# A score store and a probability load as three transfers of 32 rows each

## The chip, the cores and the metric

The kernel runs on one core of a Trainium2 chip. A core has five engines that run their own instruction streams side by side: TensorE (PE, matrix products into PSUM), VectorE (DVE), ScalarE (ACT), GpSimd (POOL) and SyncE (SP), which here does nothing but issue DMA transfers and wait. They meet at semaphores. The metric is the device time of one execution in microseconds, lower is better. Before the change it was 2473.29 us, the median of 3 runs (2472.25 to 2475.6).

## The reference

Two cross-attention layers are applied to `x` of 64 batches, 256 positions, 320 channels, 20 heads of 16. Each batch has 77 context tokens of 512 features. Layer 0 uses all 77 as text. Layer 1 takes the first 73 as text and the last 4 as image tokens, whose scores get a cosine term. Cut to what matters here, in layer 1:

```python
q = heads(hidden_states @ W_q)
probs_t = softmax(q . (text @ W_k) * Dh ** -0.5)
text_out = probs_t @ (text @ W_v)
attn_scores = jnp.einsum('bhsd,bhnd->bhsn', q, k_ip) * attn_scale     # 4 image tokens
qsem = l2norm(jnp.einsum('bhst,bte->bhse', probs_t, text_ehs))
sem = jnp.einsum('bhse,bne->bhsn', qsem, l2norm(ip_ehs))
probs_ip = softmax(attn_scores + 0.5 * sem, axis=-1) * spatial_mask[None, None, :, None]
ip_out = jnp.einsum('bhsn,bhnd->bhsd', probs_ip, v_ip)
out = (text_out + ip_out) @ W_out + b_out + residual
```

## The kernel before, in words

A first stage computes keys, values and the products of context tokens for all batches and leaves them in device memory; it ends at about 337 us of the span. The second stage, the function `attention`, is a software pipeline over the 64 batches, written out in full. In each round every engine works through a fixed list of steps, the table `ORDER` (L124). A word such as `1pl/4` is step `pl` of layer 1, for the batch 4 rounds back. No scheduler moves anything at run time: an engine that waits holds all that stands behind it. PSUM banks are handed from use to use by the table `USES`.

The image tokens' path in layer 1 goes as follows. TensorE computes the scores of three groups of channels (`ip_scores`, L1048), each group 32 rows (8 heads times 4 tokens) by 256 positions. ScalarE writes them to `sipst`, 96 rows of 1 KB (L1147). The softmax needs another layout, 96 rows of (head and quarter of the positions) with the 4 tokens side by side, and the turn goes through device memory: SP stores `sipst` to `s_dram` (step `ss`, L886) and loads `sip` from there (step `sl`, L891). DVE runs the image softmax in 20 small steps (`ip_softmax`, L1204). The first (L1221) needs the norms that SP has loaded (`nl`), the last writes `pip` (L1262). SP stores `pip` to `p_dram` (step `ps`, L897) and loads it as `pt`, again three groups of 32 rows (step `pl`, L902). TensorE multiplies `pt` with the image values (`attend_ip`, L1064, products of L1070), and DVE adds that to the text's result (L1269).

Around these steps SP has, in a round: the layer-0 sums of the softmax, 4 rows of `ust` to the 96 rows of `den` (step `ds`, L840), the same for layer 1 behind `pl`, the keys and the Gram matrix, two stores of the inverses (`rw`, L865), four moves of the numerators within `ust` (`sh`, L855) and the spread of the inverses over 128 rows, `rb` (`rl`, L871). DVE's reciprocal (L1195) waits for `den`. GpSimd's product with the inverses (L1310) waits for `rb`. ScalarE rounds the product to 16 bits (`ah`, L1159), GpSimd takes the rest (`al`, L1315), and TensorE's output projection (L933) needs both. DVE adds the residual to it (L1280); in layer 0 that is `x1a` or `x1b`, the input of layer 1.

Of the kernel before, what the change touches and what calls it, by code (L numbers as in the profile page):

```python
# [16 lines left out]
B, S, C = 64, 256, 320  # L17
# [7 lines left out]
CW = 3  # L25
# [6 lines left out]
SLOT = 32  # L32
# [640 lines left out]
def attention(nc, psum, early, x, k_dram, v_dram, g_dram, c_dram, kip_dram, vip_dram, r_dram, n_dram, s_dram, p_dram,  # L673
# [3 lines left out]
    with ExitStack() as stack:  # L677
        def sb(name, shape, dt=F32):
            return stack.enter_context(nc.sbuf_tensor(name, shape, dt))

        def sem(name):
            return stack.enter_context(nc.semaphore(name))
# [36 lines left out]
        sipst = sb("sipst", [IPR, 2, S])  # L719
# [4 lines left out]
        pt = sb("pt", [IPR, S])  # L724
# [11 lines left out]
        s_ss, s_sl = sem("ip_scores_stored"), sem("ip_scores_loaded")  # L736
        s_ps, s_pt = sem("ip_probabilities_stored"), sem("ip_probabilities_loaded")
# [17 lines left out]
        def banks(l, use, n=1):  # L755
            r = turn_banks.bank(l, use)
            return psum[:, r:r + n, :]
# [4 lines left out]
        def wait_free(eng, l, b, *uses):  # L762
            turn_banks.wait(eng, freed, b, l, *uses)
# [31 lines left out]
        def _(sp):  # L795
# [89 lines left out]

            def store_ip_scores(l, b, n):  # L886
                b.reached(sp, s_sip, 1, 1)
                dst = s_dram[b.parity()].rearrange("m (c s) -> c m s", c=CW)
                sp.dma_start(dst, sipst[:, b.parity(), :]).then_inc(s_ss, 16)

            def load_ip_scores(l, b, n):  # L891
                b.reached(sp, s_y, STEPS, SIP_READ - STEPS)
                b.reached(sp, s_ss, 16, 16)
                src = s_dram[b.parity()].rearrange("(n h) (q i) -> (h q) n i", n=IP, i=QS)
                sp.dma_start(sip[:, b.parity(), :, :], src).then_inc(s_sl, 16)

# [4 lines left out]

            def load_ip_probabilities(l, b, n):  # L902
                b.reached(sp, s_ps, 16, 16)
                src = p_dram.rearrange("m (c s) -> c m s", c=CW)
                sp.dma_start(pt[:], src).then_inc(s_pt, 16)

            def store(l, b, n):
                b.reached(sp, s_xo[1], 1, 1)
# [4 lines left out]
                               "vi": load_vip, "ds": move_denominators, "d": move_semantics, "sh": move_numerators,  # L913
                               "rw": store_inverses, "rl": spread_inverses, "ns": store_norms, "nl": load_norms,
                               "ss": store_ip_scores, "sl": load_ip_scores, "ps": store_ip_probabilities,
                               "pl": load_ip_probabilities, "st": store})
            sp.wait_ge(s_store, 16 * B)

        @block.tensor
        def _(pe):  # L920
# [143 lines left out]
            def attend_ip(l, b, n):  # L1064
                wait_free(pe, l, b, "p")
                b.reached(pe, s_vb, 1, 1)
                b.reached(pe, s_pt, 16, 16)
                for c in range(CW):
                    rows = slice(c * SLOT, (c + 1) * SLOT)
                    mm = pe.matmul(banks(l, "p", 3)[:, c, 0:S], vb[rows, :, :].rearrange("p h d -> p (h d)"),  # L1070
                                   pt[rows, :], start=True, stop=True)
                mm.then_inc(f_p, 1)

            def output(l, b, n):
# [3 lines left out]

            program("pe", {"q": query, "s": scores, "m": turn_max, "t": turned_scores, "a": attend,
                               "u": gram_products, "n": square_norms, "i": ip_scores, "p": attend_ip, "o": output})  # L1080

        @block.scalar
# [416 lines left out]
```

## Time and profile before

| | |
|---|---|
| runs | 2473.29 us median (2472.25 to 2475.6) |
| profiled execution, its own time | 2473.34 us |
| its span | 2471.8 us |
| granted TensorE clock, mean | 0.98 |
| busy: PE, DVE, ACT, POOL | 92%, 69%, 70%, 64% |
| DMA: packets, bytes | 337787, 310.89 MB |

The span is what the profile covers; the 1.5 us between it and the execution's own time lie around it. TensorE is busy nearly all the time, but the end of its matmuls is modelled, and the other engines wait for it and it for them in turn. A share of busy time does not say what a change of one transfer is worth. For that one reads which wait ends last at a place.

### The profile page before, as it was taken

What the parts mean: (1) busy time and instruction counts of PE and PEld (TensorE: products, weight loads), DVE (VectorE), ACT (ScalarE), POOL (GpSimd) and SP (SyncE); (2) the same over time, 40 slices, a digit from 0 to 9 for tenths busy, and PEclk for the clock granted to TensorE, in tenths of its full rate; (3) what the DMA queues carried; (4) which work ended last, traced back from release to release, by engine and by line L of the source; (5) the groups of instructions that cost most, each with busy time, mean ns of one, the idle gap of its engine ahead of it and who ended that gap; (6) DMA issues with size and microseconds to landing.
All of it is one profiled execution on the core that took longest, in us unless ns stands there. A gap on an engine that the chain in (4) does not pass through costs nothing.

```text
span 2471.8 us, 90321 instructions
## 1 busy us (share of the span) xinstructions
PE 2273.8 (92%) x35896; PEld 1458.5 (59%) x35896; DVE 1699.8 (69%) x2860; ACT 1726.8 (70%) x2602; POOL 1593.7 (64%) x1056
## 2 busy tenths in 40 slices
PE   7899967999999999999999999999999999999984
PEld 5677744555555555556555555655556555556552
DVE  5534333777777777777777777777777777777763
ACT  3323325877777777778777778877787787787862
POOL 3212124777777777777777777777777777777762
PEclk9999978999999999999999999999999999999997
DMA  9677642444434444444444444444444444444431
GB/s 289 197 225 229 198 115 64 112 114 115 111 109 117 115 114 117 115 118 116 112 117 116 114 115 119 117 111 116 114 118 116 113 118 118 115 118 117 112 90 56
DMA packets 337787, 310.89 MB, mean 126 GB/s; under 512 B 180208, under 2 KB 280816, under 8 KB 337392
## 3 DMA queue, kind: packets, MB, share of 16 engines
q1 hardware_dynamic: 337392, 305.36, 44.0%
q8 instruction: 280, 4.59, 0.8%
q14 instruction: 115, 0.94, 0.1%
HBM read 164.66 MB, written 105.98 MB: 109 GB/s over the span
## 4 chain that ended last, share of the span: by engine, by line
PE 34%; DVE 18%; DMA 12%; ACT 8%; issue 6%; SPq 6%; POOL 1%; ACTq 0%; DVEq 0%; POOLq 0%
PE psum L933 8%; PE psum L1032 8%; DMA den<-ust 8%; PE psum L1016 6%; PE psum L995 5%; ACT ef L1121 5%; DVE mneg L1180 3%; DVE e L1202 2%; PE psum L936 2%; DVE sq L1221 2%; DVE ust L1269 2%; DVE outt L1280 2%; DMA pt<-p_dram 2%; PE psum L999 1%; PE psum L958 1%
## 5 line engine op out<-in xcount | busy, mean ns | idle before, releaser
L1348 POOL TENSOR_TENSOR e<-ef,eh 73x1024 f32<-73x1024 f32 x320 | 681.4, 2130 | 298.9 <-ACT eh L1136 261.9
L1121 ACT ACTIVATE ef<-psum 73x1024 f32<-73x1024 f32 (+1 forms) x640 | 628.5, 1012 | 104.8 <-PE psum L999 100.9
L1202 DVE TENSOR_TENSOR e<-psum,e 73x1024 f32<-73x1024 f32 x320 | 386.6, 1208 | 158.5 <-PE psum L1032 158.2
L1180 DVE TENSOR_REDUCE mneg<-psum 128x8 f16<-128x616 f32 (+3 forms) x512 | 448.2, 930 | 31.0 <-PE psum L958 30.2
L1032 PE MATMUL psum<-eh,gram 128*73 128x512 f16 x1280 | 337.6, 387 | 36.6 <-ACT ef L1121 12.7
L1016 PE MATMUL psum<-ef,values 128*32 128x256 f32 x5120 | 363.5, 389 | 8.0 <-DVE pip L1262 5.9
L995 PE MATMUL psum<-q_high,keys 32*73 32x256 f16 (+2 forms) x6144 | 325.5, 259 | 33.9 <-DVE mneg L1180 25.4
L1136 ACT ACTIVATE eh<-ef 73x1024 f16<-73x1024 f32 x320 | 337.0, 1053 | 16.4 <-ACT ef L1121 0.8
L995 PEld LDWEIGHTS psum<-q_high,keys 32*73 32x73 f16 (+1 forms) x6144 | 187.7, 111 | 143.6 <-issue 68.1
L1129 ACT ACTIVATE ust<-psum 128x512 f32<-128x512 f32 x384 | 228.2, 594 | 63.2 <-PE psum L1016 59.2
L1315 POOL TENSOR_TENSOR al<-ust,ah 128x768 f16<-128x768 f32 x128 | 210.7, 1646 | 86.6 <-ACT ah L1159 86.5
L1310 POOL TENSOR_TENSOR ust<-ust,rb 128x768 f32<-128x768 f32 x128 | 231.8, 1811 | 24.7 <-DMA rb<-r_dram 24.5
L1032 PEld LDWEIGHTS psum<-eh,gram 128*73 128x73 f16 x1280 | 121.5, 115 | 187.4 <-ACT ef L1121 43.8
L933 PE MATMUL psum<-ah,wo 128*128 128x256 f16 x1280 | 195.2, 276 | 16.0 <-POOL al L1315 15.8
L999 PE MATMUL psum<-mt,sel 32*73 32x256 f16 (+3 forms) x3072 | 205.7, 252 | 0.0
L995 PE MATMUL psum<-q_low,keys 32*73 32x256 f16 (+3 forms) x3072 | 205.7, 252 | 0.0
L1016 PEld LDWEIGHTS psum<-ef,values 128*32 128x32 f32 x5120 | 134.2, 110 | 113.8 <-issue 30.0
L1195 DVE RECIPROCAL rd<-den 96x64 f32<-96x64 f32 x128 | 69.7, 544 | 167.7 <-DMA den<-ust 163.4
L1044 PE MATMUL psum<-e,pick 128*32 128x256 f32 x2560 | 178.2, 388 | 3.0 <-DVE e L1202 3.0
L1187 DVE SCALAR_TENSOR_TENSOR q_low<-psum,q_high 128x640 f16<-128x640 f32 x128 | 102.2, 799 | 111.8 <-ACT q_high L1103 111.3
L933 PE MATMUL psum<-xh,wq 128*128 128x256 f16 x1024 | 156.3, 276 | 10.6 <-POOL xl L1305 4.7
L660 POOL TENSOR_TENSOR ch<-cx,one 128x2464 f16<-128x2464 f32 x7 | 30.0, 4292 | 194.4 <-PE psum L422 183.3
(180 smaller groups left out, 4659.7 us busy)
## 6 DMA issues: line engine op xcount, KB each, us to landing
rb<-r_dram SPq DMA_DIRECT2D x128, 384.0 KB, 3.8
keys<-k_dram SPq DMA_DIRECT2D x128, 231.0 KB, 3.7
values<-v_dram SPq DMA_DIRECT2D x128, 192.5 KB
ust<-ust SPq DMA_DIRECT2D x512, 48.0 KB, 2.1
v_dram<-vst SPq DMA_DIRECT2D x64, 320.0 KB
out<-outt SPq DMA_DIRECT2D x64, 320.0 KB, 2.3
k_dram<-kst SPq DMA_DIRECT2D x32, 616.0 KB, 3.9
x<-in_x SPq DMA_DIRECT2D x32, 384.0 KB, 3.7
```

Of the source, the lines that this page charges most:

```text
L933: mm = pe.matmul(o[:, c * S:(c + 1) * S], a, data[:, k, :], **at_ends)
L995: pe.matmul(o, keys(l, low, c)[rows, e, 0:n], q[rows, cols], start=(low == 0 and q is qh[l]), stop=False)
L999: mm = pe.matmul(o, sel[rows, k, 0:n], mt[l][rows, lead:lead + many], start=False, stop=True)
L1016: mm = pe.matmul(row(l, f"a{c}")[j * SLOT:(j + 1) * SLOT, r * S:(r + 1) * S], va[l][:, h, :], e, start=True, stop=True)
L1032: mm = pe.matmul(banks(l, f"u{k}", 2)[0:n, r, :], gm[:, half, :], e, start=(half == 0), stop=(half == 1))
L1121: act.activation(ef[l][0:m, unit_heads(n), :].rearrange("t h s -> t (h s)"), src, ACT.Exp, scale=SM).then_inc(s_exp[l], 1)
L1129: act.activation(ust[l][:, b.parity(), :, c, :], src, ACT.Copy).then_inc(s_u[l], 1)
L1136: act.activation(eh[0:m, unit_heads(k), :], ef[1][0:m, unit_heads(k), :], ACT.Copy, scale=0.5)\
L1180: dve.tensor_reduce(dst, o, AX_X, ALU.max, negate=True).then_inc(s_max[l], 1)
L1202: dve.tensor_tensor(rest, banks(l, f"u{k}", 2)[0:m, :, :], rest, ALU.mult).then_inc(s_wr, 1)
L1310: pool.tensor_tensor(at(l, b), at(l, b), rb[l][:], ALU.mult).then_inc(s_at[l], 1)
L1348: pool.tensor_tensor(e2[0:m, k, :, :], ef[1][0:m, unit_heads(k), :], eh[0:m, unit_heads(k), :], ALU.subtract).then_inc(s_e2, 1)
```

## The change

Where one transfer of three groups (in `s_dram` and `p_dram` a group is 256 of the 768 columns) stood, three transfers of 32 rows each stand. They raise the same semaphore, so its waits go by 48 in place of 16: in `load_ip_scores` on SP and in `attend_ip` on TensorE.

```diff
             def store_ip_scores(l, b, n):
                 b.reached(sp, s_sip, 1, 1)
-                dst = s_dram[b.parity()].rearrange("m (c s) -> c m s", c=CW)
-                sp.dma_start(dst, sipst[:, b.parity(), :]).then_inc(s_ss, 16)
+                for c in range(CW):
+                    sp.dma_start(s_dram[b.parity()][:, c * S:(c + 1) * S], sipst[c * SLOT:(c + 1) * SLOT, b.parity(), :])\
+                      .then_inc(s_ss, 16)
 
             def load_ip_scores(l, b, n):
                 b.reached(sp, s_y, STEPS, SIP_READ - STEPS)
-                b.reached(sp, s_ss, 16, 16)
+                b.reached(sp, s_ss, 16 * CW, 16 * CW)
...
             def load_ip_probabilities(l, b, n):
                 b.reached(sp, s_ps, 16, 16)
-                src = p_dram.rearrange("m (c s) -> c m s", c=CW)
-                sp.dma_start(pt[:], src).then_inc(s_pt, 16)
+                for c in range(CW):
+                    sp.dma_start(pt[c * SLOT:(c + 1) * SLOT, :], p_dram[:, c * S:(c + 1) * S]).then_inc(s_pt, 16)
...
             def attend_ip(l, b, n):
                 wait_free(pe, l, b, "p")
                 b.reached(pe, s_vb, 1, 1)
-                b.reached(pe, s_pt, 16, 16)
+                b.reached(pe, s_pt, 16 * CW, 16 * CW)
```

On SP, in a round of the loop, the score store stands between the values of layer 0 and the load of the scores, and before the change reads:

```order
L821 DMA values<-v_dram 77x640 [waits filled_a0]
L889 DMA s_dram<-sipst 3x32x256 [waits ip_scores_read]
L895 DMA sip<-s_dram 96x4x64 [waits ip_scores_stored,ip_softmax_steps]
L875 DMA rb<-r_dram_0 128x1x768 [waits inverses_stored1,text_attended1]
L862 DMA ust<-ust 16x768 [waits semantics_moved,denominators_moved1,text_attended1]
```

and after it:

```order
L821 DMA values<-v_dram 77x640 [waits filled_a0]
L889 DMA s_dram<-sipst 32x256 [waits ip_scores_read]
L889 DMA s_dram<-sipst 32x256 x2
L896 DMA sip<-s_dram 96x4x64 [waits ip_scores_stored,ip_softmax_steps]
L875 DMA rb<-r_dram_1 128x1x768 [waits inverses_stored1,text_attended1]
```

Nothing changes its place; two more transfers stand ahead of the load that waits for all three. Further down in the same round on SP, from the sums of layer 0 to the spread of its inverses (`rb`), before the change:

```order
L845 DMA den<-ust 96x1x64 [waits inverses0,sums_read0]
L821 DMA values<-v_dram 77x640 [waits filled_a1]
L905 DMA pt<-p_dram 96x1x256 [waits ip_probabilities_stored]
L845 DMA den<-ust 96x1x64 [waits inverses1,sums_read1]
L814 DMA keys<-k_dram 128x924 [waits filled_t0]
L828 DMA gram<-g_dram 77x146 [waits filled_u]
L869 DMA r_dram_1<-rd 8x12x64 [waits inverses0]
L869 DMA r_dram_1<-rd 8x12x64
L862 DMA ust<-ust 16x768 [waits denominators_moved0,text_attended0]
L862 DMA ust<-ust 16x768 x3
L875 DMA rb<-r_dram_1 128x1x768 [waits inverses_stored0,text_attended0]
```

and after it:

```order
L845 DMA den<-ust 96x1x64 [waits inverses0,sums_read0]
L821 DMA values<-v_dram 77x640 [waits filled_a1]
L906 DMA pt<-p_dram 32x256 [waits ip_probabilities_stored]
L906 DMA pt<-p_dram 32x256 x2
L845 DMA den<-ust 96x1x64 [waits inverses1,sums_read1]
L814 DMA keys<-k_dram 128x924 [waits filled_t0]
L828 DMA gram<-g_dram 77x146 [waits filled_u]
```

Here too the order stays, with two more transfers between the first of `pt` and the sums of layer 1; what stands behind them follows as before. On the other engines no instruction is added or moved.

## Rows read from the trace of the kernel before

**Rows 1.** The page: the chain that ended last, by line.
```profile
PE psum L933 8%; PE psum L1032 8%; DMA den<-ust 8%; PE psum L1016 6%; PE psum L995 5%; ACT ef L1121 5%; DVE mneg L1180 3%; DVE e L1202 2%; PE psum L936 2%; DVE sq L1221 2%; DVE ust L1269 2%; DVE outt L1280 2%; DMA pt<-p_dram 2%; PE psum L999 1%; PE psum L958 1%
```

**Rows 2.** Timeline of SP in one batch: start, duration, queue, line, transfer, count.
```profile
1513.23 0.64 SPq L845 DMA_DIRECT2D den<-ust  x1
...
1514.46 0.74 SPq L905 DMA_DIRECT2D pt<-p_dram  x1
1515.30 0.58 SPq L845 DMA_DIRECT2D den<-ust  x1
...
1518.41 2.49 SPq L862 DMA_DIRECT2D ust<-ust  x4
1521.00 0.56 SPq L875 DMA_DIRECT2D rb<-r_dram  x1
```

**Rows 3.** Timeline of DVE in that batch; in brackets the idle time before.
```profile
1515.56 0.54 DVE L1195 RECIPROCAL rd<-den 96x64 f32<-96x64 f32 x1
...
1519.60 0.55 DVE L1195 RECIPROCAL rd<-den 96x64 f32<-96x64 f32 x1 [2.42 <-DMA den<-ust]
...
1529.40 0.74 DVE L1221 TENSOR_SCALAR sq<-n 96x64 f32<-96x64 f32 x1
...
1533.53 0.96 DVE L1280 SCALAR_TENSOR_TENSOR x1a<-psum,res 128x768 f32<-128x768 f32 x1
```

**Rows 4.** Timeline of GpSimd (POOL) in that batch.
```profile
1525.54 1.80 POOL L1310 TENSOR_TENSOR ust<-ust,rb 128x768 f32<-128x768 f32 x1
1528.44 1.65 POOL L1315 TENSOR_TENSOR al<-ust,ah 128x768 f16<-128x768 f32 x1 [1.10 <-ACT ah L1159]
```

**Rows 5.** Timeline of ScalarE (ACT) in that batch.
```profile
1527.46 0.84 ACT L1159 ACTIVATE ah<-ust 128x768 f16<-128x768 f32 x1 [0.60 <-POOL ust L1310]
```

**Rows 6.** Line 1221 over the run: count, duration in ns min/median/max.
```profile
L1221 DVE TENSOR_SCALAR sq<-n x64: 180/847/2076, 443.4 to 2442.7; 96x64 f32<-96x64 f32 x64
```

**Rows 7.** Line 875 (rb) over the run: who waited (us, times), and its landings.
```profile
  POOL ust L1310: 24.5, 11
...
DMA to landing us min/median/max: 3.5/3.8/5.3
```

**Rows 8.** Issues of five kinds, ns min/median/max; last, the landings of L895.
```profile
L889 SPq DMA_DIRECT2D s_dram<-sipst x64: 759/780/822, 411.9 to 2421.3; - x64
L905 SPq DMA_DIRECT2D pt<-p_dram x64: 713/722/862, 459.2 to 2454.0; - x64
L862 SPq DMA_DIRECT2D ust<-ust x512: 507/589/1787, 366.6 to 2449.2; - x171
L798 SPq DMA_DIRECT2D kip<-kip_dram x2: 595/598/600, 337.4 to 338.0; - x2
L895 SPq DMA_DIRECT2D sip<-s_dram x64: 321/343/354, 416.6 to 2424.8; - x64
...
DMA to landing us min/median/max: 1.9/2.0/4.5
```

**Rows 9.** Busy time in one microsecond (columns: PE, PEld, DVE, ACT, POOL, clock, DMA, GB/s).
```profile
1504.00:1505.00 1.00, 1.00 (x20) 0.42 (x24) 1.00 (x2) 0.82 (x1) 1.00 (x1) 1.00 0.16 53
```

**Rows 10.** The chain that ended last, in order of time: start, us, what.
```profile
1515.30 4.17 DMA den<-ust
...
2421.28 3.42 DMA s_dram<-sipst
...
2453.99 4.14 DMA pt<-p_dram
```

**Rows 11.** SP's own waits over the run: us in total, times, longest us.
```profile
SPq L121 <- DMA s_dram<-sipst: 198.7, 63, 4.0
SPq L845 <- ACT ust L1129: 195.9, 62, 24.1
...
SPq L879 <- ACT nst L1142: 44.2, 49, 5.8
...
SPq L905 <- DMA p_dram<-pip: 7.2, 7, 1.7
```

## The prediction

> **What bounds the kernel now.** I read the chain of waits first. Its list by line [rows 1] names no owner: five matmul lines, ACT's exponential and one transfer, den<-ust, share it. So the loop is a ring through all engines, and what matters is which link ends last at each place. The pt loads of the 64 batches lie between 459.2 and 2454.0 us [rows 8], so a batch takes 31.7 us, and I read one batch engine by engine. The sync queue (SP) comes first [rows 2], because both edits are there. SP waits for the layer-0 sums, issues den<-ust of layer 0 (1513.23), the values, pt (1514.46), den<-ust of layer 1 (1515.30), and then works on without a wait through the four ust moves to the spread of layer 0's inverses, rb<-r_dram (1521.00). From 1513.23 to 1521.56 SP is bound by issuing: whatever one issue costs more, all behind it starts later by as much.
>
> Two chains leave that stretch. The first is den<-ust of layer 1: DVE's reciprocal stands 2.42 us for it [rows 3] and is at the head of what DVE does next. The second is rb: GpSimd's product with the inverses starts at 1525.54, ScalarE's copy ah follows at 1527.46, GpSimd's rest al at 1528.44 and ends at 1530.09 [rows 4, 5]. DVE's next step, the small operation of L1221, starts at 1529.40 and ends at 1530.14, 0.05 us behind al [rows 3]. It takes 180 ns at its shortest and 847 at the median [rows 6], so in the usual batch it is held until al is through, and behind it on DVE are the steps of the image softmax and x1a (1533.53), for which all engines wait at the next batch's start. I lined its end up with al's end in all 64 batches: in 59 it is less than 0.1 us behind. This GpSimd chain, not den, ends last in most batches. The Trainium skill ("SBUF — State Buffer", Who interferes with whom) says that a VectorE tensor_scalar in a two-port mode and a GpSimd instruction lock each other out for a whole instruction. These rows agree; nothing below needs the rule beyond them.
>
> How much room has rb? It was issued at 1521.00 and used at 1525.54, 4.54 us later. It lands 3.8 us after the issue at the median, 3.5 to 5.3 in all [rows 7], and a landing is seen about 0.1 us later, so the usual batch has 0.6 us to spare, and 11 times (8 of them in the steady part) GpSimd waits for rb already (24.5 us in all, most of it in the 3 at the ends).
>
> **The change, part by part.** Both edits replace one transfer of 96 rows of 1 KB, seen by the queue as 3 groups of 32, by three of 32 rows.
>
> *Issue time.* The one transfer costs SP 780 ns (store) and 722 ns (load) at the median [rows 8]. No row shows 32 rows. The nearest are 16 rows, 589 ns (L862, 512 times, never under 507), and 64 rows, 598 ns (L798). At the other end stands 343 ns for 96 rows in one pattern (L895) [rows 8]. I take 590, since 16 and 64 rows bracket 32 and agree; the bounds are 343 and 780. The four ust moves last 2.48 us as a group [rows 2], so 40 ns lie between two: three new issues last 3 x 0.59 + 2 x 0.04 = 1.85 us. At the pt load, den of layer 1 now follows 0.84 us after its start [rows 2]; then it would follow 1.95 us after, **1.1 us later**. Nobody on SP between pt and rb waits, so rb moves by the same 1.1.
>
> *What hides it at rb.* 0.6 of the 1.1: rb would be late by 0.5 in a usual batch and by all of 1.1 in the 8 that wait already. The GpSimd chain behind it is ready at once, ScalarE's ah already waits for it, and L1221 waits for al, so what is late there is late in x1a and in the batch. Over 60 steady batches: 52 x 0.45 + 8 x 1.1 = **+32 us**.
>
> *Landing time.* In a microsecond in which the score store is alone in flight, the DMA engines are 0.16 busy and move 53 GB/s [rows 9]. That is 3 engines of 16, 18 GB/s each; a third of the transfer, 32 KB, takes 1.85 us on one. Den of layer 0 was issued onto free engines at 1513.23 and its reciprocal runs at 1515.56, so it landed in under 2.33 us; den of layer 1, issued right behind pt, took 4.17 [rows 2, 3, 10]. The difference, 1.84, is just the third that lies ahead of it on three engines. The skill ("DMA: Bandwidth & Descriptors", Why a DMA increments its semaphore by 16 and not by 1) says that a transfer runs on the largest number of engines up to 16 that divides the slowest dimension of both sides. The 0.16 agrees with 3; by the rule 32 rows would run on 16.
>
> With 16 engines, 2 rows each, the last of three lands about 2.0 us after its issue, as sip (96 KB) does [rows 8]: 1.26 + 2.0 = 3.3 us after the group's start. Then
> - the store lands at 3.3 in place of 4.0 (0.78 of issue, and SP waits 198.7 us for it, 3.2 a batch [rows 11]), and what is behind it on SP (sip, rb of layer 1, the moves, x, p_dram<-pip) starts 0.7 us sooner. Nearly all of it only lengthens SP's next wait, for ScalarE's sums (195.9 us, 3.2 a batch [rows 11]). What counts is that p_dram is stored sooner: 7 times the pt load waits for it, 7.2 us [rows 11]. 7 x 0.5 gives **-3.5 us**.
> - pt lands at 3.3 in place of 4.1 or more. In the loop TensorE has other products to do until then. In the last batches nothing hides it: the chain holds pt three times, the last at 4.14, and the store at 3.42 [rows 10]. 3 x 0.8 + 0.1 gives **-2.5 us**.
> - den of layer 1 lands at 1.95 + 2.33 + 0.3 = 4.6 after pt's start in place of 5.0: 0.4 sooner in spite of the later issue. I count 0: where it ends last the GpSimd chain is within 0.1 to 0.2 us of it, and that one now ends later.
>
> Behind rb SP's next wait is for ScalarE's nst (44.2 us, 49 times, 0.9 each [rows 11]), so nearly all of the 1.1 us ends there and don't reach the semantics' moves.
>
> **Sum.** 32 - 3.5 - 2.5 = +26, less about 1 where another chain is later than rb anyway: +25 us. The profiled execution took 2473.34 us (span 2471.8 and 1.5 around it), the median of the runs is 2473.29, so the same number serves: 2498 us.
>
> **Rivals.**
> *A, the short issue.* If 32 rows cost what 96 in one pattern do, 0.34 us, the group lasts 1.1 us and rb moves by 0.35: hidden in the usual batch, and 8 x 0.35 + a few more = +5 us, against -6. Time 2472, no change. For it: L895. Against it: nothing of 64 rows or fewer is under 0.5. It decides below about 0.38 us an issue.
> *B, not slower, clearly faster.* The late rb doesn't reach the end because L1221 is only drawn out in the record and another chain (through TensorE's output projection) sets x1a with room to spare; den's sooner landing then pays what the first chain shows, up to 0.1 us a batch, and with the two gains the sum is -6 - 6: 2461 to 2467. Against it: 59 of 64 times L1221 ends with al, and the record shows x1a's step running as soon as the steps behind L1221 are through.
> *C, the landing doesn't change.* If den's 4.17 us come from the values and keys beside it and not from pt's third, it still takes 4.1 us but starts 1.1 later, and DVE's reciprocal, which has about 0.2 us to spare against the GpSimd chain, moves the ring by about 0.9 a batch: +55, 2528. The skill's rule for two transfers to disjoint partition halves ("DMA: Bandwidth & Descriptors", Rules for kernel authors: "Don't bother") points this way; but it compares halves that each use all engines, and here one group uses three. The match of 1.84 with 1.85 speaks against C.
> *D, issues as dear as now.* With 0.72 each the group lasts 2.24, rb moves by 1.5: 52 x 0.9 + 8 x 1.5 - 6 = +53, 2526.
>
> **Chances.** The forecast 0.62, A 0.2, B 0.06, C 0.06, D 0.06. Its own range is 2487 to 2510 (issues of 0.53 to 0.65 us). The range with A is 2469 to 2510; C, D and B are left out. A difference under 0.2% (5 us) can't be told from none here. Faster: B and a small part of A, 0.08. Same: the rest of A and the lowest end of the forecast, 0.2. Slower: 0.72.
>
> **What would show it.** The new load's issues at 0.55 to 0.62 us each; den of layer 1 issued 1.9 to 2.0 us after the first of them and landed after about 2.6; rb issued 7.6 us after pt in place of 6.5; GpSimd's L1310 waiting for rb in most batches, about 30 us more; L1221 longer by as much; DVE's wait for den gone or halved; SP's wait for s_dram about 2 us a batch; TensorE's wait for pt in the last batches shorter. It is wrong if the three issues last under 1.3 us, or if GpSimd waits for rb and the batches still take 31.7 us.

## The result, and the profile after it

| | us, median | lowest to highest | runs |
|---|---|---|---|
| before | 2472.11 | 2467.5 to 2475.6 | 8 |
| after | 2478.19 | 2475.13 to 2485.74 | 8 |

The ratio is 1.0027, 95% interval 1.0015 to 1.0040. The change costs 6.1 us where 25 were forecast. The sign is right and the size is a quarter of the forecast. The time lies inside the range only because rival A was taken into it; the forecast's own part of it began at 2487. The profiled execution of the kernel after took 2475.13 us (span 2473.5), 3 us less than its median, so its span is only 1.7 us above that of before: the two traces show where time moved, but less than a third of the difference itself. Lines from 890 on have moved down by one: L905 is L906, L1221 is L1222.

The chain that ended last, by line, in the page of the kernel after:

```profile
PE psum L1033 10%; PE psum L934 9%; PE psum L1017 7%; PE psum L996 6%; ACT ef L1122 4%; ACT q_high L1104 3%; PE psum L937 3%; DVE e L1203 2%; SPq L862 2%; DVE sq L1222 2%; DVE mneg L1181 2%; DVE outt L1281 2%; DMA n_dram<-nst 2%; PE psum L1000 2%; DMA rb<-r_dram 2%
```

The 8% of den<-ust [rows 1] is gone without any gain in time. Other links stand in its place, among them the sync queue's moves (L862), rb and the store of the semantics' sums (n_dram<-nst). Whoever had read the 8% as 190 us to be won would have been wrong by all of it.

The issues of the two split transfers, in ns (min/median/max), over the run of the kernel after; the last line belongs to the load:

```profile
L889 SPq DMA_DIRECT2D s_dram<-sipst x192: 324/418/1547, 410.4 to 2424.2; - x192
...
L906 SPq DMA_DIRECT2D pt<-p_dram x192: 312/416/1287, 457.5 to 2458.1; - x192
...
DMA to landing us min/median/max: 1.6/2.3/4.0
```

Against [rows 8] one transfer of 780 or 722 ns became three of about 0.42 us. The load's first takes 0.33, the two behind it 0.42 each, and some 0.04 lie between two, so the load's group lasts 1.25 us at the median (the store's 1.29), not 1.85. This is the forecast's mis-sized number.

SP's timeline, answering to [rows 2], first in an ordinary batch, then in one of those that cost time:

```profile
1512.64 1.24 SPq L906 DMA_DIRECT2D pt<-p_dram  x3
1513.98 0.56 SPq L845 DMA_DIRECT2D den<-ust  x1
1514.58 0.47 SPq L814 DMA_DIRECT2D keys<-k_dram  x1
1515.10 0.38 SPq L828 DMA_DIRECT2D gram<-g_dram  x1
...
1519.62 0.56 SPq L875 DMA_DIRECT2D rb<-r_dram  x1
```

```profile
1480.37 1.25 SPq L906 DMA_DIRECT2D pt<-p_dram  x3
1481.72 0.57 SPq L845 DMA_DIRECT2D den<-ust  x1
1482.34 0.47 SPq L814 DMA_DIRECT2D keys<-k_dram  x1
1482.85 1.30 SPq L828 DMA_DIRECT2D gram<-g_dram  x1
...
1488.30 0.56 SPq L875 DMA_DIRECT2D rb<-r_dram  x1
```

Den of layer 1 follows the load's start by 1.34 us (0.84 before). rb follows it by 6.98 in the ordinary batch and by 7.93 in the other, because there the Gram load's issue takes 1.30 us in place of 0.38. GpSimd in the same two batches, now the costly one first; in brackets the idle time before:

```profile
1492.08 1.82 POOL L1311 TENSOR_TENSOR ust<-ust,rb 128x768 f32<-128x768 f32 x1 [0.55 <-DMA rb<-r_dram]
...
1524.17 1.81 POOL L1311 TENSOR_TENSOR ust<-ust,rb 128x768 f32<-128x768 f32 x1
```

In the costly batch rb is used 3.78 us after its issue, as soon as it is there, and GpSimd has stood 0.55 us. In the ordinary one it is used 4.55 us after and was there before. So the ordinary batch still has its room, and the batch with the long issue has none left.

What the landings give back, over the run (us, times): DVE's wait for den, TensorE's for pt; the third line is GpSimd's wait for rb.

```profile
  DVE rd L1196: 75.0, 65
...
  PE psum L1071: 11.6, 1
...
  POOL ust L1311: 35.7, 32
```

Den's wait was 163.4 us in 65 waits before. The reciprocal in this batch shows what is left of the 2.42 [rows 3]:

```profile
1516.20 0.55 DVE L1196 RECIPROCAL rd<-den 96x64 f32<-96x64 f32 x1 [0.85 <-DMA den<-ust]
```

It starts 2.22 us after den's issue, where 4.30 lay between them before. GpSimd's wait for rb rose from 24.5 us in 11 waits [rows 7] to 35.7 in 32. SP's own waits, answering to [rows 11]:

```profile
SPq L845 <- ACT ust L1130: 217.6, 64, 22.4
...
SPq L121 <- DMA s_dram<-sipst: 120.5, 63, 3.7
SPq L884 <- DMA n_dram<-nst: 71.6, 60, 2.6
...
SPq L879 <- ACT nst L1143: 17.3, 20, 7.0
...
SPq L906 <- DMA p_dram<-pip: 4.9, 7, 1.5
```

SP's wait for the score store (the line of L121) fell from 3.2 to 1.9 us a batch. Of these 1.2 us some 0.5 are only the group's longer issue. The next wait, for ScalarE's sums, took 21.7 us more over the run (195.9 to 217.6), 0.3 a batch, so less of the rest went there than the forecast's "nearly all". SP's slack before the store of the semantics' sums, 44.2 us in 49 waits, is down to 17.3 in 20: the later issues have eaten it. Behind it DVE's L1222 waits more often for the semantics' sums n:

```profile
L1222 DVE TENSOR_SCALAR sq<-n x64: 180/968/1796, 441.8 to 2445.3; 96x64 f32<-96x64 f32 x64
...
  DMA n<-n_dram: 12.4, 12
```

Before, it waited 6.0 us in 2 waits.

A reading batch by batch (61 batches of the steady part, from the timelines): rb is issued 8.01 us on average after den of layer 0 before the change and 8.53 after, 0.52 later. GpSimd waits for rb 5.7 us in 9 of the batches before, 17.6 in 31 after.

### The profile page after: what moved, and what is told of

Read it like the earlier page. It is cut to its first block, busy times and chain, and to the rows that moved or that the text cites. A ratio compares the mean times of both kernels' runs of the same rounds, so it can differ in the third digit from the quotient of the medians.

```text
span 2473.5 us, 90577 instructions
## 1 busy us (share of the span) xinstructions
PE 2272.9 (92%) x35896; PEld 1456.8 (59%) x35896; DVE 1717.2 (69%) x2860; ACT 1724.3 (70%) x2602; POOL 1595.6 (65%) x1056
## 4 chain that ended last, share of the span: by engine, by line
PE 39%; DVE 18%; ACT 8%; SPq 7%; issue 6%; DMA 6%; POOL 2%; ACTq 0%; DVEq 0%; POOLq 0%
PE psum L1033 10%; PE psum L934 9%; PE psum L1017 7%; PE psum L996 6%; ACT ef L1122 4%; ACT q_high L1104 3%; PE psum L937 3%; DVE e L1203 2%; SPq L862 2%; DVE sq L1222 2%; DVE mneg L1181 2%; DVE outt L1281 2%; DMA n_dram<-nst 2%; PE psum L1000 2%; DMA rb<-r_dram 2%
## 5 line engine op out<-in xcount | busy, mean ns | idle before, releaser
L1033 PE MATMUL psum<-eh,gram 128*73 128x512 f16 x1280 | 337.9, 387 | 44.2 <-DVE x1b L1281 15.0
L1311 POOL TENSOR_TENSOR ust<-ust,rb 128x768 f32<-128x768 f32 x128 | 232.3, 1815 | 36.3 <-DMA rb<-r_dram 35.7
L1160 ACT ACTIVATE ah<-ust 128x768 f16<-128x768 f32 x128 | 107.4, 839 | 88.0 <-POOL ust L1311 79.1
L934 PEld LDWEIGHTS psum<-ah,wo 128*128 128x128 f16 x1280 | 118.8, 98 | 62.0 <-issue 26.3
```

The costliest lines, as they stand in the source:

```text
L934: mm = pe.matmul(o[:, c * S:(c + 1) * S], a, data[:, k, :], **at_ends)
L1033: mm = pe.matmul(banks(l, f"u{k}", 2)[0:n, r, :], gm[:, half, :], e, start=(half == 0), stop=(half == 1))
L1311: pool.tensor_tensor(at(l, b), at(l, b), rb[l][:], ALU.mult).then_inc(s_at[l], 1)
```

## The experiments

**Theory R:** the price is what SP issues ahead of rb, the load's two more transfers; the store's two stand in a wait and cost nothing, and its sooner landing gains. Against it stand a price of more transfers wherever they are issued, and a price that comes with the store's part; each expectation names its rivals. Each ratio is against runs of the kernel before that were timed beside it (of its three medians in the table the first goes with e1 to e4, the second with e6 to e9, the third with e5 and e11; the kernel after has the pair of the section on the result). A ratio is of medians, and its interval is of 95%. The columns on the right are of each one's trace over the whole run (us, times). Some 18 us of GpSimd's wait are one wait ahead of the first batch, and 11.6 to 13.2 us of TensorE's are one wait in the last batch; every kernel has both. A trace is of one execution, which can lie off the median: 4.5 us above it in e1, 6.8 above in e11, 4.3 below in e8, 8.2 above in e5.

| kernel | us | ratio | interval | GpSimd for rb | DVE for den | TensorE for pt |
|---|---|---|---|---|---|---|
| before | 2471.6, 2472.0, 2470.9 | 1 | | 24.5, 11 | 163.4, 65 | 19.1, 15 |
| after | 2478.2 | 1.0027 | 1.0015–1.0040 | 35.7, 32 | 75.0, 65 | 11.6, 1 |
| e1 load only | 2481.1 | 1.0038 | 1.0023–1.0053 | 47.4, 34 | 78.9, 63 | 11.6, 1 |
| e2 store only | 2468.5 | 0.9983 | 0.9973–0.9992 | 22.4, 9 | 161.3, 66 | 17.2, 12 |
| e3 two more ahead of rb | 2528.8 | 1.0235 | 1.0212–1.0257 | 80.4, 58 | 155.3, 64 | 21.3, 21 |
| e4 two more in the wait | 2472.8 | 1.0008 | 0.9998–1.0019 | 23.2, 13 | 165.4, 65 | 20.2, 16 |
| e5 load as six | 2571.3 | 1.0404 | 1.0384–1.0424 | 126.2, 63 | 172.3, 66 | 25.4, 29 |
| e6 after, Gram behind rb | 2467.5 | 0.9986 | 0.9975–0.9997 | 23.1, 9 | 74.5, 64 | 11.7, 1 |
| e7 store only, Gram behind rb | 2466.5 | 0.9981 | 0.9972–0.9990 | 18.3, 1 | 163.9, 66 | 19.0, 11 |
| e8 before, Gram behind rb | 2468.8 | 0.9989 | 0.9979–0.9999 | 18.4, 2 | 159.8, 66 | 19.6, 10 |
| e9 before, den ahead of pt | 2474.4 | 1.0007 | 0.9998–1.0016 | 21.8, 8 | 21.9, 9 | 32.6, 39 |
| e11 e6 with den ahead of pt | 2477.2 | 1.0028 | 1.0015–1.0040 | 31.7, 22 | 22.4, 11 | 15.7, 11 |

**e1 and e2: each edit alone.** The wait for the split transfer's semaphore goes with it, as in the change; these lines are left out of the cuts.

```
e1, against before:
-                src = p_dram.rearrange("m (c s) -> c m s", c=CW)
-                sp.dma_start(pt[:], src).then_inc(s_pt, 16)
+                for c in range(CW):
+                    sp.dma_start(pt[c * SLOT:(c + 1) * SLOT, :], p_dram[:, c * S:(c + 1) * S]).then_inc(s_pt, 16)
e2, against before:
-                dst = s_dram[b.parity()].rearrange("m (c s) -> c m s", c=CW)
-                sp.dma_start(dst, sipst[:, b.parity(), :]).then_inc(s_ss, 16)
+                for c in range(CW):
+                    sp.dma_start(s_dram[b.parity()][:, c * S:(c + 1) * S], sipst[c * SLOT:(c + 1) * SLOT, b.parity(), :])\
+                      .then_inc(s_ss, 16)
```

> Only the probability load is three transfers; the score store stays one. Theory R (the extra issue time of the load makes rb, the spread of layer 0's inverses, late): rb 0.5 us later after the layer-0 sums than before, GpSimd's wait for rb in about 30 batches; +9 us in the loop, some -3.5 in the last batches where pt lands sooner: +5.5 us, 2478. Rival N (each of the 128 extra transfers costs the same wherever it stands, as through SP's stalls or the DMA engines' packets): half of the change's +6, so +3 us, 2475. Rival S (the store is what costs): 0 or less, 2469 to 2472.

> Only the score store is three transfers; the probability load stays one. Theory R: no issue is added between the layer-0 sums and rb, so rb keeps its time; the pt load's 7 waits for p_dram (7.2 us) mostly go: -3.5 us in the loop, -0.5 at the end: 2468. Rival N: +3 us, 2475. Rival S: +6 us, 2478.

The load costs 9.5 us, 4 more than expected; the store gains 3.1 us by the medians and 4.2 by the ratio. Their sum is the change's own price within the intervals. So the price does not come with the store's part. The store's gain is clear of the noise, since its interval ends at 0.9992.

**e3 and e4: the same two small transfers in two places of SP's order**, ahead of rb and in the wait for the sums.

```
e3:  ... 0ds/1 1v/2 1pl/4 1ds/3 1z/4 0k/0 1g/2 ...
e4:  ... 1ps/4 1z/4 0ds/1 1v/2 1pl/4 1ds/3 0k/0 1g/2 ...
both:
+            def spare_loads(l, b, n):
+                b.reached(sp, s_spare, 32, 0)
+                for c in (0, 1):
+                    sp.dma_start(spare[c * SLOT:(c + 1) * SLOT, :], x[0, c, 0:SLOT, :]).then_inc(s_spare, 16)
```

> The kernel before, with two more loads of 32 rows of the input into an unused tile in every batch, issued right behind the layer-1 sums and so ahead of rb; nobody uses their data. Theory R: at 0.42 to 0.46 us an issue rb comes 0.9 us later; by the room that rb has in the batches of before (0.6 us at the median) that is +25 us (20 to 30), 2497. Rival N: +6 us, 2478.

> The same two loads as in the run with two more ahead of rb, issued between the store of the probabilities and the layer-0 sums, where SP waits 3.2 us a batch for ScalarE. Theory R: the wait hides them: 0 to +1 us, 2472 to 2473. Rival N: +6 us as in that run, 2478.

Two more transfers ahead of rb cost 57 us; the same two in the wait cost 1 to 2, not told from none. A price of the number of transfers as such falls. The 57 is over twice my number. SP and GpSimd in one batch of e3:

```profile
1499.54 0.58 SPq L847 DMA_DIRECT2D den<-ust  x1
1500.16 0.93 SPq L917 DMA_DIRECT2D spare<-in_x  x2
1501.14 0.42 SPq L816 DMA_DIRECT2D keys<-k_dram  x1
1501.61 1.53 SPq L830 DMA_DIRECT2D gram<-g_dram  x1
...
1507.30 0.56 SPq L877 DMA_DIRECT2D rb<-r_dram  x1
```

```profile
1511.63 1.82 POOL L1318 TENSOR_TENSOR ust<-ust,rb 128x768 f32<-128x768 f32 x1 [1.77 <-DMA rb<-r_dram]
```

The pair occupies 0.98 us of SP, and here the Gram load is 1.53 long in place of 0.38. On average over the 61 steady batches rb is issued 1.2 us later after den of layer 0 than before and used 0.91 later, and 0.91 over 61 batches is 55 us, near the 57 measured. The same sum doesn't give every price: in e1 rb is used 0.35 later, which would be 21 us, and 9.5 were measured (12 between the two spans). e3 hands nothing back either: den and pt arrive as late as before. In 35 of its 61 batches such a long issue stands ahead of rb (16 of 61 before).

**e5: the load as six transfers of 16 rows.**

```
-                for c in range(CW):
-                    sp.dma_start(pt[c * SLOT:(c + 1) * SLOT, :], p_dram[:, c * S:(c + 1) * S]).then_inc(s_pt, 16)
+                for r in range(2 * CW):
+                    c, h = divmod(r, 2)
+                    sp.dma_start(pt[r * 16:(r + 1) * 16, :], p_dram[h * 16:(h + 1) * 16, c * S:(c + 1) * S]).then_inc(s_pt, 16)
```

> The kernel after with the pt load as six transfers of 16 rows in place of three of 32. Theory R with the issue time measured in the kernel after (0.42 us an issue behind another one): the group lasts 2.5 us in place of 1.25, den of layer 1 and rb are issued 1.25 us later still, 1.8 us later than in the kernel before. Two more issues ahead of rb (1.33 us) cost 57 us; from there each 0.1 us costs 6 us, so +85 against before: 2555, range 2540 to 2570, with GpSimd waiting for rb in all batches. Rival I (16 rows cost the 0.59 us of the ust moves whatever side they read): the group lasts 3.6 us, rb 2.9 us later, 2620. Rival N (an issue's time goes with its bytes, half the rows half the time): the group lasts 1.3 us and the time stays at 2478.

```profile
L907 SPq DMA_DIRECT2D pt<-p_dram x384: 302/420/1859, 456.8 to 2562.6; - x192
...
DMA to landing us min/median/max: 1.6/2.0/3.4
```

The wait in `attend_ip` goes by 96 here. It costs 100 us, between R's 85 and I's 150 and 1.3 us over R's range. An issue of 16 rows takes 0.42 us, just as one of 32: in this form neither the rows nor the bytes set it, so both rivals of its text fall. The four moves of L862 have 16 rows too and take 0.59, so their price isn't that of their rows. The group takes 2.64 us at the median; rb comes 2.26 us later than before on average, not 1.8, as my number left out the gaps between issues and the long ones. GpSimd waits for it in all 61 batches.

**e6, e7 and e8: the Gram load moved from ahead of rb to behind it**, in the kernel after, the one with the store alone, and the one before.

```
-  ... 1pl/4 1ds/3 0k/0 1g/2 0rw/1 0sh/1 0rl/1 1c/1
+  ... 1pl/4 1ds/3 0k/0 0rw/1 0sh/1 0rl/1 1g/2 1c/1
```

> The kernel after, with the one transfer between the pt load and rb that nobody needs soon, the load of the Gram matrix, moved behind rb in SP's order. The load split alone cost 9.5 us, and rb was issued 0.5 us later in the kernel after. Theory R (what counts is how much SP issues ahead of rb): without the Gram load, some 0.4 us with its gap, rb is issued at nearly the same place as before the change, GpSimd waits for it in about 10 batches in place of 31, and 5 to 8 us of time come back: 2470 to 2473 against 2478 for the kernel after, a ratio to the kernel before of 0.999 to 1.0005. Rival G (the Gram load was where it was needed): TensorE waits for it at its layer-1 work, and the time stays at 2478 or more. Rival S (what makes the change slower is the periodic long issue on SP or the number of issues as such): no change from 2478, since the count is the same.

> The kernel before with only the store split into three, which measured 0.9983, and the load of the Gram matrix moved behind rb. Theory R: the rb waits that this kernel still has (7 batches, some 4 us) go, and the gain of the store stays: 2464 to 2466, ratio 0.997. Rival G: TensorE waits for the Gram matrix, 2470 or more.

> The kernel before with the load of the Gram matrix moved behind rb and nothing else. Theory R: rb is issued 0.4 us sooner, by the slacks of before its 8 late batches lose most of their 4.2 us: 2467 to 2469, ratio 0.998 to 0.999. Rival G: TensorE waits for the Gram matrix, ratio over 1.001. It also tells what the moved load does apart from the two splits.

This is the decisive test: e6 has all the transfers of the kernel after and the same waits for den and pt, and what stands between the keys and the Gram load's new place comes sooner: the stores of the inverses, the moves and rb (7.99 us after den of layer 0 on average, as the 8.01 of before). The price of the change is gone: 2467.5, 10.7 us under the kernel after, more than the 5 to 8 expected. Moving the Gram load by itself is worth 3.3 us (e8), and rb is then waited for in one batch only. The fair pair for the change is therefore e6 against e8, both with the Gram load late: there the two splits cost nothing (2467.5 against 2468.8), where they cost 6.1 us with it early. In none of the three does TensorE wait for the Gram matrix, so Rival G falls, and with e6 the rival that blames the count of issues, which is the same there. e7 has the lowest median, 0.9981 of before, a little short of the 0.997 expected. Its interval overlaps those of e2, e6 and e8. All four are faster than both kernels (against before, e6 and e8 by little more than their intervals), and which of them is best isn't told apart. With rb sooner, the load's split shows neither gain nor price: e6 and e7 differ by it and by 1.0 us, within their intervals.

**e9: den of layer 1 ahead of the pt load**, both splits undone.

```
-  ... 1v/2 1pl/4 1ds/3 0k/0 ...
+  ... 1v/2 1ds/3 1pl/4 0k/0 ...
```

> The kernel before with the store of layer 1's sums (den<-ust) issued ahead of the pt load in place of behind it; both splits undone. It tells what made den take 4.17 us. Theory Q (den stood behind pt's 32 KB on each of three DMA engines): issued ahead, it lands in about 2.2 to 2.4 us, DVE's wait for it (163 us in all, some of it as the first thing ended) falls to 75 us or less, as with the split load. Rival C (the values and keys beside it made it slow): it still takes about 4. Both: rb is issued at the same place, so the rb waits don't change. The time: den's late landing was 0.39 us a batch on DVE's q_low but TensorE's ring hid it mostly; pt is issued 0.6 us later, and lands later by as much. 2470 to 2474, ratio 0.999 to 1.001, if the image products aren't waiting for pt; the split's part beyond rb is then no more than that.

DVE's wait for den falls from 163.4 us to 21.9, so it was the pt load ahead of it that made den take 4.17 us, and not the values or keys, which still stand beside it. Forecast rival C falls. The time doesn't move. But e9 isn't den's gain alone: pt is issued later, and TensorE's wait for it rose from 19.1 us in 15 waits to 32.6 in 39. The chain that ended last goes through den<-ust 47 times between 400 us and the end in the kernel before. In e9 it goes through pt<-p_dram 38 times instead. The page's list by line of e9:

```profile
PE psum L933 9%; PE psum L1032 9%; DMA pt<-p_dram 7%; PE psum L1016 7%; PE psum L995 6%; ACT ef L1121 5%; DVE mneg L1180 2%; PE psum L936 2%; PE psum L1044 2%; DVE e L1202 2%; PE psum L958 2%; ACT q_high L1103 2%; PE psum L999 2%; DVE outt L1280 2%; SPq L845 2%
```

**e11: e6 with den ahead of the pt load.**

```
-  ... 1v/2 1pl/4 1ds/3 0k/0 0rw/1 ...
+  ... 1v/2 1ds/3 1pl/4 0k/0 0rw/1 ...
```

> Both splits, the load of the Gram matrix behind rb, and den of layer 1 issued ahead of the pt load. Putting den ahead of the grouped load made TensorE wait for pt 39 times in place of 15 and cost about 2 us. Theory: split in three the load lands about 0.7 us sooner, which is more than the 0.56 us that den ahead delays it, so TensorE waits for pt in hardly any batch, and den's remaining wait (75 us in all, some 1 us a batch but behind ScalarE) goes too: 2464 to 2468. Rival (three starts later by 0.56 us still arrive too late): TensorE waits for pt 20 times or more, 2469 to 2472.

A miss: 2477.2, 10 us over e6, though TensorE's waits for pt stayed few (11) and den's wait went. GpSimd waits for rb 22 times in place of 9, 8.6 us more. In its trace the long issues fall into the stretch ahead of rb in 25 of 61 batches, 22.9 us over the usual length in sum, against 13 and 9.7 us in e6. They hold 10.9 of its 12.8 us of rb waits in these batches. What the rest of the 10 us comes from stays open, and so does whether the order of the two issues moves the long ones there or chance does: this is one profiled execution of each, and that of e11 is one of its four slowest, at 2483 to 2485 us, while its other eight runs took 2472 to 2477.

## Why the forecast had the sign and not the size

**Issue time: the step that failed.** The prediction took 590 ns for a transfer of 32 rows because 16 and 64 rows "bracket 32 and agree". Measured are 0.33 for the first and 0.42 for the others. The number of rows wasn't what sets it, as e5 shows. The trace of before had transfers between DRAM and SBUF that were cheap: the 343 ns of L895 (96 rows of 4 pieces) [rows 8], which the prediction saw and set aside, and this one, a plain block like the new ones, which it doesn't name:

```profile
L910 SPq DMA_DIRECT2D out<-outt x64: 333/344/362, 476.4 to 2469.0; - x64
```

So the group lasted 1.25 us in place of 1.85, and rb moved by 0.46 us at the median and 0.52 on average in place of 1.1. The prediction had named this as what would make it wrong ("three issues last under 1.3 us"). The term of +32 us is the one that was mis-sized. Its mechanism holds. Its count, one room of 0.6 us for all batches but 8, does not at this size: it would hide a shift of 0.52 in the other 52 and leave 8 x 0.52 = 4 us, less 6 for the gains: -2, no slowdown at all. The room has to be taken batch by batch. With the room that each of 60 steady batches of the kernel before had at rb (use less landing, less 0.1), a shift of 0.52 gives 9 us and one of 1.1 gives 37. So that the sign came out right is owed in part to the issue time being put too high. Rival A was said to decide below 0.38 an issue. The measured 0.42 lies between A and the forecast, and so does the time.

**The room of rb.** It is 0.6 us in the usual batch, as said, and hides a shift of 0.46 in most of them. What isn't hidden is mostly in the batches in which one of SP's issues ahead of rb takes 0.25 us or more over its usual length. Of 61 steady batches of the kernel after 22 are such, and they hold 13.9 of the 17.6 us that GpSimd waits for rb. In e1 they are 26, with 22.5 us of 28.6. Before the change they were 16, with 4.4 us of 5.7. So long issues were there before; the half microsecond took away the room that had hidden them.

**Behind rb** the prediction let nearly all of the lateness end in SP's wait for nst. Most of it did: that slack of 0.9 us a batch was largely used up (44.2 to 17.3 us in all), and the store n_dram<-nst is issued only 0.14 us later on average. But it also lands 0.3 us later after its issue (3.06 in place of 2.74), so the load n<-n_dram is issued 0.5 us later, and the chain of the kernel after goes 11 times through this store and load, such as here, in the batch with the long Gram issue:

```profile
1482.85 1.30 SPq L828
...
1489.49 3.59 DMA n_dram<-nst
1493.09 2.23 DMA n<-n_dram
```

It goes 8 times through rb. Thus a second way by which the stretch's length reaches the end was missed. How the 6.1 us divide between the two wasn't measured. In e6 the Gram load stays ahead of the semantics' store, the load of n is still issued 0.3 us later than in the kernel before, and yet the whole price goes, which speaks for rb as the larger.

**The store's gain** was put at 3.5 us and is 3 to 4 (e2). The reason given was fewer waits for p_dram. In e2, where the store's split stands alone, they fell from 7.2 us in 7 waits to 3.1 in 3, which fits; in the kernel after only to 4.9, and in e7 to 6.1 though it is no slower than e2. So the reason is open. That the store lands sooner is plain: SP's wait for it fell by 1.2 us a batch. Two microseconds of its flight in the kernel after (columns as in [rows 9]):

```profile
1501.00:1502.00 1.00, 0.92 (x4) 0.38 (x4) 0.93 (x4) 1.00 (x2) 0.82 (x1) 1.00 0.64 168
1502.00:1503.00 1.00, 1.00 (x17) 0.42 (x16) 1.00 (x2) 0.79 (x1) 0.87 (x1) 1.00 0.39 132
```

These can't be set against the 0.16 and 53 GB/s of [rows 9] as they stand, because packets of 2560 bytes, which are of other transfers (the values' load and the output's store), are in both. The packets of 1 KB alone tell it, counted in the traces: in 58 batches of the kernel before at most 4 to 6 of the store's 96 were under way at one time, in the kernel after 8 to 15. For the load it is the same (4 to 6, then 8 to 15). The Trainium skill ("DMA: Bandwidth & Descriptors", Why a DMA increments its semaphore by 16 and not by 1) ties the number of engines to what divides the slowest dimension, 3 before and 32 now. The counts agree that more engines work now; they don't give their number. But the store's packets take no less time from the first to the last, 1.75 us at the median against 1.59. They begin 0.95 us after the group's start in place of 1.95, and there lies its whole gain. The load's take 1.56 against 2.50 and begin after 1.07 in place of 1.71.

The Trainium skill ("DMA: Bandwidth & Descriptors", Rules for kernel authors) advises against two transfers to disjoint partition halves, because both halves spread over all 16 engines anyway. For this store the split pays all the same: e2 is faster, with an interval that leaves out 1. The advice supposes a whole transfer that already uses all engines, and this one did not.

**Den of layer 1** was expected 0.4 us sooner after the load's start and counted as nothing. In the batches shown its reciprocal starts 3.56 us after the load's start where 5.14 lay before [rows 2, 3]: 1.58 sooner, as the issue is only 0.5 later and what follows it 2.1 shorter. Counting it as nothing fits the runs (e6 against e7, e9), but none has den sooner and nothing else changed.

**Pt in the last batches** was put at −2.5 us. TensorE's waits for pt fell from 19.1 us to 11.6, and that by the load's split alone (e1); the one in the last batch went from 13.1 to 11.6. What it was worth in time isn't shown: e6, which has the split, isn't faster than e7, but it also waits for rb 4.9 us more.

**The sum with the measured size:** 9 for rb less 4 for the store is 5, with nothing for pt, against 6.1 measured. e1 less e2's gain is 5.3 to 6.4.

## What to carry to other kernels

- In a queue whose issues run back to back, a split transfer costs its extra issues times their length, at whatever chain starts behind them. Put it where the queue waits anyway, or move something that nobody needs soon behind the urgent one. Moving one load gave back more than the whole change cost.
- A single link's share in the chain that ended last isn't what its removal gains: here den's 8% went from the chain in six kernels (after, e1, e5, e6, e9, e11), each time other links took its place, and in e9 the time stayed. What tells is the room of the second chain, batch by batch, with its spread and not its median.
- For the price of an operation that the trace doesn't show, look for a neighbour in form (the pattern of its rows, which memories it joins) as well as the neighbour in size, and if the two disagree, carry both through the sum. Here the plain block of L910 at 0.34 was nearer than the moves of 16 rows at 0.59.

## What was not expected of the hardware

SP's issue of a transfer takes 0.25 to 1.6 us more than usual now and then, on many lines: the Gram load 1.30 in place of 0.38, one load of x 1.71 in place of 0.52. In the kernel after there are 104 such in the 2479 issues after 380 us (78 us in all), before 72 in 2223 (50 us). Most fall outside the stretch ahead of rb: in the kernel after 15 of the 78 us are in it.

The traces tell what goes with them. The queue q8 of the page, of kind "instruction", moves packets of 16 KB (280 of them in either kernel, 266 after 380 us), each under way for about 1.1 us. Of the 104 long issues 101 overlap one of these packets, of the other 2375 issues 382 do; before the change it is 70 of 72 and 422 of 2151. A long issue mostly ends 0.3 to 0.4 us behind the end of its packet. In the costly batch shown above the packet is under way from 1482.88 to 1483.76, and the Gram load's issue lasts from 1482.85 to 1484.15. This is the queue's line for 1482.8 to 1484.2 us:

```profile
q8 instruction: 1, 0.02, 3.9%
```

The overlap alone isn't enough. In the ordinary batch a packet is under way from 1514.27 to 1515.56, over the issues of den, the keys and the Gram matrix, and none of them is longer. No run moved these packets, so that they cause the long issues is likely from the counts but not shown.

A transfer of 1 KB rows costs SP 0.33 us as the first and 0.42 behind another of its kind, with 32 rows or 16, against 0.72 to 0.78 as one of 3 groups of 32. So the split transfer isn't three times as dear to issue, but 1.7 times.
